# A graph attention kernel: 98 columns of one sum move from GpSimd to VectorE, and the vector loop is written out

## The chip, the cores and the metric

The kernel runs on one core of a Trainium2 chip. The metric is the device time of one execution in microseconds (us), lower is better. It was taken in 3 runs before the change. One more execution was taken with the hardware profiler.

Engines are named as in the profile: PE is the matrix engine (PEld its weight loads), DVE the vector engine, ACT the scalar engine, POOL the GpSimd engine, SP the queue that starts transfers.

## The reference

The model is a two-layer graph attention network followed by a soft mixture of experts. There are 1250 nodes with 768 features, 41250 edges (self loops included), 8 heads of 128 channels in the first attention layer and one head of 768 in the second. The change touches the attention layers alone:

```
def gat_layer(x, W, att_src, att_dst, bias, src, dst, heads, out_ch, concat):
    h = (x @ W.T).reshape(n, heads, out_ch)
    a_src = einsum('nhc,hc->nh', h, att_src)
    a_dst = einsum('nhc,hc->nh', h, att_dst)
    e = leaky_relu(a_src[src] + a_dst[dst], 0.2)
    m = segment_max(e, dst)
    ex = exp(e - m[dst])
    alpha = ex / (segment_sum(ex, dst)[dst] + 1e-16)
    out = segment_sum(alpha[:, :, None] * h[src], dst)
    return out + bias

x = x + gat2(relu(gat1(layernorm(x))))
x = x + soft_moe(layernorm(x))
```

## The kernel before, in words

The kernel makes the attention dense. A first stage counts the edges between every pair of nodes and keeps `ln_c`, the logarithm of the count, with a large negative number where there is no edge: 10 tiles of 128 destination nodes by 1280 source nodes. 1250 nodes are padded to `NP` = 1280, so the last 30 columns of each row belong to no node.

`attend` then runs once for each layer. It has `heads * NT` steps: 80 in the first layer (`gat1`), 10 in the second (`gat2`). One step is one tile of 128 destinations for one head. A step goes through the engines so:

- POOL (L737) adds `s_row`, the source logits of the head spread over all partitions, and the tile's `ln_c`, into `base`, 128x1280.
- ACT (L753) makes `relus`, the part that turns the sum into a leaky ReLU.
- DVE (L783) adds `relus` and `base` into `q` and takes the row maximum in the same instruction; a second short instruction of that line reads the maximum out into `top`. Ahead of it a MEMSET of one column, `gate` (L782), carries the last of the waits. L787 negates `top`.
- ACT (L758) takes the exponential of `q` in place and sums it into `den`. DVE turns the sum into a factor (L806, L810).
- PE (L849) transposes `q` into PSUM as `gat_pt`, ten blocks of 128x128. ACT (L768) and DVE (L798) copy it out as a high and a low fp16 half, `pt_hi` and `pt_lo`.
- PE (L79 to L81) multiplies by the features `h` in three products, `gat_o`. DVE (L818 in the first layer, L830 and L834 in the second) scales it and adds the bias, into `rows`. In the first layer PE transposes `rows` (L854) and ACT (L763) and DVE (L792) write the result as fp16 halves.

All engines run the same counter `k` from -1 to `steps + 2`, each with its own lag. In iteration `k`, POOL, ACT and DVE work on `base`, `relus` and `q` of step `k + 1`; DVE then does the low half of step `k - 1`, the rows of step `k - 2` and the factor of step `k`. `base`, `relus` and `q` have two slots each. POOL may start `base` of step `k + 1` when `q` of step `k - 1` is done:

```
at_least(eng, q_ready, k)
eng.tensor_tensor(base[:, w, :], ..., ALU.add).then_inc(base_ready, 1)
```

The order on every engine is that of the code. It is made short by `rolled`: iterations -1 to 4 are written out, those up to `steps - 2` run in a hardware loop of two iterations a turn (37 turns in the first layer, 2 in the second), and the last four are written out again. In the loop the semaphore values and addresses come from registers, which the engine's own queue works out (`DVEq`, `POOLq` rows in the profile).

Of the kernel before, what the change touches and what calls it, by code (L numbers as in the profile page):

```python
# [24 lines left out]
F32 = mybir.dt.float32  # L25
# [5 lines left out]
ds = bass.ds  # L31
# [38 lines left out]
def at_least(eng, sem, value):  # L70

    if not isinstance(value, int) or value > 0:
        eng.wait_ge(sem, value)
# [567 lines left out]
def attend(nc, mem, sem, const, name, heads, width, ln_c, h, nad, a_rows, bias, turned=None,  # L641
# [8 lines left out]

    steps = heads * NT
    s_row = mem("s_row", [P, 2, NP], F32)
    relus = mem("relus", [P, 2, NP], F32)
    base = mem("base", [P, 2, NP], F32)
    q = mem("q", [P, 2, NP], F32)
    pt = [mem(f"pt_{x}", [P, 2, NT, P], F16) for x in ("hi", "lo")]
    top = mem("top", [P, 2], F32)
    neg_top = mem("neg_top", [P, 2], F32)
    gate = mem("gate", [P, 2], F32)
    den = mem("den", [P, 4], F32)  # L660
    scaled = mem("scaled", [P, 2], F32)
    factor = mem("factor", [P, 2], F32)
# [1 line left out]
    bias_all = mem("bias_all", [P, heads * width], F32)  # L664
    in_bias, bias_ready = sem(f"{name}_in_bias"), sem(f"{name}_bias")
    in_s = sem(f"{name}_in_s")
    relu_ready, base_ready, q_ready = sem(f"{name}_relu"), sem(f"{name}_base"), sem(f"{name}_q")
    neg_ready, p_ready = sem(f"{name}_neg"), sem(f"{name}_p")
    pt_turned, hi_ready, lo_ready = sem(f"{name}_ptt"), sem(f"{name}_hi"), sem(f"{name}_lo")
    out_done, scaled_ready, factor_ready = (  # L670
# [8 lines left out]
    with (  # L679
# [5 lines left out]
        def run(eng, step):  # L685
            rolled(eng, step, -1, 5, steps - 1, steps + 3)
# [7 lines left out]
        @block.sync  # L694
        def _(eng):
            eng.dma_start(bias_all[:, :], bias.to_broadcast([P, heads * width])).then_inc(in_bias, 16)

            def load_s(head, slot):
                at_least(eng, in_s, 16 * head)

                at_least(eng, relu_ready, (head - 1) * NT)
                at_least(eng, base_ready, (head - 1) * NT)
                eng.dma_start(s_row[:, slot, :].rearrange("p (t n) -> p t n", t=NT),
                              a_rows[ds(head * NT, NT), :].unsqueeze(0).to_broadcast([P, NT, P]))\
                   .then_inc(in_s, 16)

            for head in range(min(heads, 2)):
                load_s(head, head)
            if heads > 2:
                with eng.Fori(1, heads // 2) as pair:  # L710
                    for slot in range(2):
                        load_s(2 * pair + slot, slot)
            if residual is not None:
                def load_x(k):
                    eng.dma_start(xs[:, k % 2, :], residual[k * P:(k + 1) * P, :])\
                       .then_inc(in_x[k % 2], 16)

                load_x(0)
                load_x(1)
                for k in range(steps):  # L720
                    eng.wait_ge(rows_ready, k + 1)
                    eng.dma_start(stored[k * P:(k + 1) * P, :], rows[:, k % 2, :])\
                       .then_inc(saved[k % 2], 16)
                    if k + 2 < steps:
                        load_x(k + 2)
                for u in range(2):
                    eng.wait_ge(saved[u], 16 * (steps // 2))

        @block.gpsimd
        def _(eng):  # L730
            def step(k, u):
                if valid(k + 1):
                    w = (u + 1) % 2
                    head, j = head_tile(k + 1)
                    eng.wait_ge(in_s, 16 * (head + 1))
                    at_least(eng, q_ready, k)
                    eng.tensor_tensor(base[:, w, :], s_row[:, ds(head % 2, 1), :],  # L737
                                      ln_c[:, ds(j, 1), :], ALU.add).then_inc(base_ready, 1)
            run(eng, step)

        @block.scalar
        def _(eng):
            eng.wait_ge(in_bias, 16)
            eng.activation(bias_all[:, :], bias_all[:, :], ACT.Copy, scale=out_scale)\
               .then_inc(bias_ready, 1)

            def step(k, u):
                w = (u + 1) % 2
                if valid(k + 1):
                    head, j = head_tile(k + 1)  # L750
                    eng.wait_ge(in_s, 16 * (head + 1))
                    at_least(eng, q_ready, k)
                    eng.activation(relus[:, w, :], s_row[:, ds(head % 2, 1), :], ACT.Relu,  # L753
                                   bias=nad[:, ds(k + 1, 1)], scale=-0.8).then_inc(relu_ready, 1)
                if valid(k):
                    eng.wait_ge(neg_ready, k + 1)
                    at_least(eng, factor_ready, k - 1)
                    eng.activation(q[:, u, :], q[:, u, :], ACT.Exp, bias=neg_top[:, u:u + 1],  # L758
                                   accum_out=den[:, u:u + 1]).then_inc(p_ready, 1)
                if turned and valid(k - 3):  # L760
                    head, j = head_tile(k - 3)
                    eng.wait_ge(rows_turned, k - 2)
                    eng.activation(turned[0][:, ds(head, 1), ds(j * P, P)],  # L763
                                   op[:, w, P:2 * P], ACT.Relu).then_inc(th_ready, 1)
                if valid(k - 1):
                    eng.wait_ge(pt_turned, k)
                    at_least(eng, out_done, k - 2)
                    eng.activation(pt[0][:, w, :, :].rearrange("p t n -> p (t n)"),  # L768
                                   tp[:, w, 0:NP], ACT.Copy, scale=S_PROB).then_inc(hi_ready, 1)
            run(eng, step)  # L770

        @block.vector
        def _(eng):
            eng.wait_ge(bias_ready, 1)

            def step(k, u):
                w = (u + 1) % 2
                if valid(k + 1):
                    eng.wait_ge(relu_ready, k + 2)
                    eng.wait_ge(base_ready, k + 2)  # L780
                    at_least(eng, pt_turned, k)
                    eng.memset(gate[:, w:w + 1], 0.0)  # L782
                    eng.tensor_tensor_reduce(q[:, w, :], relus[:, w, :], base[:, w, :], 1.0, -MASK / 2,  # L783
                                             ALU.add, ALU.max, top[:, w:w + 1]).then_inc(q_ready, 1)
                    eng.wait_ge(q_ready, k + 2)
                    at_least(eng, p_ready, k)
                    eng.tensor_scalar(neg_top[:, w:w + 1], top[:, w:w + 1], -1.0, None, ALU.mult)\  # L787
                       .then_inc(neg_ready, 1)
                if turned and valid(k - 3):
                    head, j = head_tile(k - 3)  # L790
                    eng.wait_ge(th_ready, k - 2)
                    eng.scalar_tensor_tensor(turned[1][:, ds(head, 1), ds(j * P, P)],  # L792
                                             op[:, w, P:2 * P], 0.0,
                                             turned[0][:, ds(head, 1), ds(j * P, P)],
                                             ALU.max, ALU.subtract).then_inc(tl_ready, 1)
                if valid(k - 1):
                    eng.wait_ge(hi_ready, k)
                    eng.scalar_tensor_tensor(pt[1][:, w, :, :].rearrange("p t n -> p (t n)"),  # L798
                                             tp[:, w, 0:NP], S_PROB,
                                             pt[0][:, w, :, :].rearrange("p t n -> p (t n)"),  # L800
                                             ALU.mult, ALU.subtract).then_inc(lo_ready, 1)
                if valid(k - 2):
                    rows_out(k - 2, u)
                if valid(k):
                    eng.wait_ge(p_ready, k + 1)
                    eng.tensor_scalar(scaled[:, u:u + 1], den[:, u:u + 1], S_PROB * S_ACT / out_scale,  # L806
                                      TINY, ALU.mult, ALU.add).then_inc(scaled_ready, 1)
                    eng.wait_ge(scaled_ready, k + 1)
                    at_least(eng, rows_ready, k - 1)
                    eng.reciprocal(factor[:, u:u + 1], scaled[:, u:u + 1]).then_inc(factor_ready, 1)  # L810

            def rows_out(k, u):
# [7 lines left out]
                       .then_inc(rows_ready, 1)  # L820
                else:

                    if isinstance(k, int):
                        eng.wait_ge(in_x[u], 16 * (k // 2 + 1))
                    else:
                        eng.wait_ge(in_x[u], 16 * ((k - u) // 2 + 1))
                    if not isinstance(k, int) or k >= 2:

                        eng.wait_ge(saved[u], 16 * ((k - u) // 2))
                    eng.tensor_tensor(rows[:, u, :], xs[:, u, :], bias_all[:, :], ALU.add)\  # L830
                       .then_inc(sum_ready, 1)
                    eng.wait_ge(sum_ready, k + 1)
# [3 lines left out]
                                             rows[:, u, :].rearrange("p (c n) -> p c n", c=2),  # L836
                                             ALU.mult, ALU.add).then_inc(rows_ready, 1)

            run(eng, step)

        @block.tensor
        def _(eng):
            def step(k, u):
                w = (u + 1) % 2
                if valid(k):
# [748 lines left out]
```

## Time and profile before

| | us |
|---|---|
| median of 3 runs | 2096.01 (2095.04 to 2098.13) |
| the profiled execution | 2098.8 |
| its span, first to last instruction | 2097.0 |
| PE busy | 1781.3 (85%) |
| DVE busy | 1227.6 (59%) |
| ACT busy | 932.2 (44%) |
| POOL busy | 270.6 (13%) |

The span is what the trace covers; 1.8 us of the profiled execution lie around it. The shares are averages over all stages. The first attention layer runs from about 447 to 835 us after the span's start, the second from about 934 to 1075 us, and POOL works nearly only in these two. In a row of the timeline, "idle before <-releaser" is the engine's idle time ahead of the instruction and what ended it; "issue" is idle time for which the profile shows no releaser.

### The profile page before, as it was taken

How to read it: one execution, taken by the hardware profiler on the slowest of the kernel's cores; microseconds unless marked ns; L12 is line 12 of the kernel's file. 1: busy time of each engine (PE TensorE's matmuls, PEld its weight loads, DVE VectorE, ACT ScalarE, POOL GpSimd, SP SyncE). 2: the span in 40 equal slices, each digit the busy share in tenths (PEclk: the TensorE clock that was granted, in tenths of full speed). 3: DMA queues.
4: the chain of work that ended last, by engine and by line, in shares of the span. 5: the costliest groups of instructions: out<-in, count | busy, mean ns of one | idle time of the engine just before them, and what ended most of it. 6: DMA issues, size and time to landing. Idle time of an engine off the chain costs nothing. (4 is left out here: it accounts for less than half of the span.)

```text
span 2097.0 us, 38651 instructions
## 1 busy us (share of the span) xinstructions
PE 1781.3 (85%) x11825; PEld 1097.9 (52%) x11825; DVE 1227.6 (59%) x2013; ACT 932.2 (44%) x1366; POOL 270.6 (13%) x113
## 2 busy tenths in 40 slices
PE   4948878858898887958847979999999996999799
PEld 2413333336777776535533435655656553666455
DVE  6676777778888887435345114555555555666311
ACT  2107767758888886214203113333333333565300
POOL 0000000036666663013000000000000000000000
PEclk9979999979999999988978999999999998999999
DMA  4000000000000000111140001212112123332311
GB/s 156 0 7 0 0 0 0 0 35 13 13 13 25 13 0 26 50 35 46 61 170 26 0 30 62 78 59 76 62 59 79 59 71 123 113 110 74 128 64 50
DMA packets 33674, 104.08 MB, mean 50 GB/s; under 512 B 3286, under 2 KB 3386, under 8 KB 33500
## 3 DMA queue, kind: packets, MB, share of 16 engines
q1 hardware_dynamic: 33564, 103.39, 14.4%
q8 instruction: 28, 0.46, 0.1%
q14 instruction: 18, 0.15, 0.0%
q10 hardware_dynamic: 64, 0.08, 0.0%
HBM read 75.07 MB, written 28.38 MB: 49 GB/s over the span
## 5 line engine op out<-in xcount | busy, mean ns | idle before, releaser
L737 POOL TENSOR_TENSOR base<-s_row,ln_c 128x1280 f32 (+1 forms) x90 | 261.2, 2903 | 609.1 <-DMA s_row<-a_rows 440.5
L631 PE MATMUL ce_c<-one_src,one_dst 128*128 x1053 | 211.6, 347 | 42.7 <-issue 34.9
L574 DVE TENSOR_SCALAR one_src<-iota,src 128x1280 f16 x351 | 171.2, 549 | 69.3 <-PE ce_c L631 62.2
L79 PE MATMUL di_l<-x2t_hi,ph_hi 128*128 128x512 f16 (+1 forms) x576 | 196.4, 341 | 12.4 <-DVE ph_lo L1160 11.0
L80 PE MATMUL di_l<-x2t_lo,ph_hi 128*128 128x512 f16 (+1 forms) x576 | 196.3, 341 | 0.0
L81 PE MATMUL di_l<-x2t_hi,ph_lo 128*128 128x512 f16 (+1 forms) x576 | 196.3, 341 | 0.0
L79 PE MATMUL gat_o<-h_hi,pt_hi 128*128 (+1 forms) x800 | 180.0, 228 | 2.4 <-DVE pt_lo L798 1.9
L631 PEld LDWEIGHTS ce_c<-one_src,one_dst 128*128 x1053 | 101.7, 97 | 152.7 <-issue 92.2
L81 PE MATMUL gat_o<-h_hi,pt_lo 128*128 (+1 forms) x800 | 172.5, 218 | 0.0
L80 PE MATMUL gat_o<-h_lo,pt_hi 128*128 (+1 forms) x800 | 171.8, 218 | 0.0
L849 PE MATMUL gat_pt<-ident,q 128*128 128x128 f32 x900 | 121.1, 284 | 53.9 <-ACT q L758 41.9
L783 DVE CUSTOM_DVE_ANT_0 q<-relus,base 128x1280 f32<-128x1280 f32 x90 | 165.1, 1834 | 0.0
L598 ACT ACTIVATE apart<-iota,minus_dst 128x128 f16 x351 | 115.4, 391 | 71.1 <-PE ce_c L631 37.5
L768 ACT ACTIVATE pt_hi<-gat_pt 128x1280 f16<-128x1280 f32 x90 | 110.8, 1231 | 66.0 <-PE gat_pt L849 66.0
L849 PEld LDWEIGHTS gat_pt<-ident,q 128*128 128x128 f32 x900 | 101.7, 145 | 66.0 <-ACT q L758 43.4
L798 DVE SCALAR_TENSOR_TENSOR pt_lo<-gat_pt,pt_hi 128x1280 f16<-128x1280 f32 x90 | 133.3, 1481 | 1.8 <-ACT pt_hi L768 1.7
L79 PE MATMUL co_c<-ps_hi,hid_hi 128*128 128x305 f16 (+1 forms) x384 | 115.4, 301 | 20.8 <-DVE ps_lo L1387 20.2
L758 ACT ACTIVATE q<-q,neg_top 128x1280 f32<-128x1280 f32 x90 | 122.5, 1361 | 19.5 <-DVE neg_top L787 19.5
L1155 DVE SCALAR_TENSOR_TENSOR pt_lo<-di_t,pt_hi 128x1280 f16<-128x1280 f32 x32 | 47.7, 1492 | 140.5 <-ACT pt_hi L1109 140.5
L753 ACT ACTIVATE relus<-s_row,nad 128x1280 f32 (+1 forms) x90 | 122.4, 1362 | 1.9 <-DMA s_row<-a_rows 1.9
L80 PE MATMUL co_c<-ps_lo,hid_hi 128*128 128x305 f16 (+1 forms) x384 | 115.1, 300 | 0.0
L81 PE MATMUL co_c<-ps_hi,hid_lo 128*128 128x305 f16 (+1 forms) x384 | 115.1, 300 | 0.0
(214 smaller groups left out, 3656.1 us busy)
## 6 DMA issues: line engine op xcount, KB each, us to landing
logits_t<-lg SPq DMA_DIRECT2D x32, 625.0 KB, 3.7
logits_in<-logits_t SPq DMA_DIRECT2D x32, 625.0 KB, 4.0
phf<-in_phi SPq DMA_DIRECT2D x32, 384.0 KB, 3.9
xs<-x SPq DMA_DIRECT2D x20, 384.0 KB, 4.9
s_row<-a_rows SPq DMA_DIRECT2D x9, 640.0 KB, 3.8
ew<-in_fw SPq DMA_DIRECT2D x6, 768.0 KB, 13.1
wf<-in_fw SPq DMA_DIRECT2D x12, 384.0 KB, 6.8
xs<-in_x SPq DMA_DIRECT2D x10, 384.0 KB, 7.4
```

What stands on the lines that cost most here:

```text
L79: eng.matmul(out, lh, rh, start=first, stop=False, skip_group_check=True)
L80: eng.matmul(out, lh, rl, start=False, stop=False, skip_group_check=True)
L81: return eng.matmul(out, ll, rh, start=False, stop=last, skip_group_check=True)
L574: eng.tensor_scalar(one_src[:, ds(slot + i, 1), :], const["iota"][:, :], src[:, ds(block_at + i, 1)], None, ALU.is_equal)\
L598: eng.activation(apart[:, ds(k % 2, 1), i, :], const["iota"][:, j * P:(j + 1) * P], ACT.Abs, bias=minus_dst[:, ds(block_at + i, 1)])\
L631: mm = eng.matmul(cp[:, j % 2, a:a + n], one_dst[:, ds(slot + i, 1), :], one_src[:, ds(slot + i, 1), a:a + n], start=False, stop=False, sk ...
L737: eng.tensor_tensor(base[:, w, :], s_row[:, ds(head % 2, 1), :], ln_c[:, ds(j, 1), :], ALU.add).then_inc(base_ready, 1)
L753: eng.activation(relus[:, w, :], s_row[:, ds(head % 2, 1), :], ACT.Relu, bias=nad[:, ds(k + 1, 1)], scale=-0.8).then_inc(relu_ready, 1)
L758: eng.activation(q[:, u, :], q[:, u, :], ACT.Exp, bias=neg_top[:, u:u + 1], accum_out=den[:, u:u + 1]).then_inc(p_ready, 1)
L783: eng.tensor_tensor_reduce(q[:, w, :], relus[:, w, :], base[:, w, :], 1.0, -MASK / 2, ALU.add, ALU.max, top[:, w:w + 1]).then_inc(q_ready, 1)
L798: eng.scalar_tensor_tensor(pt[1][:, w, :, :].rearrange("p t n -> p (t n)"), tp[:, w, 0:NP], S_PROB, pt[0][:, w, :, :].rearrange("p t n -> ...
L849: mm = eng.transpose(tp[:, u, t * P:(t + 1) * P], q[:, u, t * P:(t + 1) * P], const["ident"][:, :])
```

## The change

In both layers the sum `base` is split: POOL adds columns 0 to 1151 (`POOL_PART` = 9 * 128), DVE adds columns 1152 to 1249, 98 of them, just ahead of its own use of `base` (new line L788). `relus`, `base`, the sum with maximum and the exponential leave the 30 pad columns out. The pads of `q`, which PE still transposes, are set to zero once by POOL, and PE waits for that once. The MEMSET of `gate` is gone. The DVE program of `attend` is no longer looped: all its iterations are written out with constants. The other engines' loops stay. Two slots of `base` and `relus` now lie 1250 columns (5000 bytes) apart, where they were 1280 apart.

```
-    relus = mem("relus", [P, 2, NP], F32)
-    base = mem("base", [P, 2, NP], F32)
+    POOL_PART = (NT - 1) * P
+    relus = mem("relus", [P, 2, N], F32)
+    base = mem("base", [P, 2, N], F32)
...
                 at_least(eng, relu_ready, (head - 1) * NT)
-                at_least(eng, base_ready, (head - 1) * NT)
+                at_least(eng, base_pool, (head - 1) * NT)
+                at_least(eng, base_dve, (head - 1) * NT)
...
         @block.gpsimd
         def _(eng):
+            for u in range(2):
+                eng.memset(q[:, u, N:NP], 0.0).then_inc(pads, 1)
+
             def step(k, u):
...
-                    eng.tensor_tensor(base[:, w, :], s_row[:, ds(head % 2, 1), :],
-                                      ln_c[:, ds(j, 1), :], ALU.add).then_inc(base_ready, 1)
+                    eng.tensor_tensor(base[:, w, 0:POOL_PART], s_row[:, ds(head % 2, 1), 0:POOL_PART],
+                                      ln_c[:, ds(j, 1), 0:POOL_PART], ALU.add).then_inc(base_pool, 1)
             run(eng, step)
+            eng.wait_ge(pads, 2)
...
                 if valid(k + 1):
+                    head, j = head_tile(k + 1)
+                    eng.wait_ge(in_s, 16 * (head + 1))
+                    at_least(eng, q_ready, k)
+                    eng.tensor_tensor(base[:, w, POOL_PART:N], s_row[:, head % 2, POOL_PART:N],
+                                      ln_c[:, j, POOL_PART:N], ALU.add).then_inc(base_dve, 1)
                     eng.wait_ge(relu_ready, k + 2)
-                    eng.wait_ge(base_ready, k + 2)
+                    eng.wait_ge(base_pool, k + 2)
+                    eng.wait_ge(base_dve, k + 2)
                     at_least(eng, pt_turned, k)
-                    eng.memset(gate[:, w:w + 1], 0.0)
-                    eng.tensor_tensor_reduce(q[:, w, :], relus[:, w, :], base[:, w, :], 1.0, -MASK / 2,
+                    eng.tensor_tensor_reduce(q[:, w, 0:N], relus[:, w, :], base[:, w, :], 1.0, -MASK / 2,
                                              ALU.add, ALU.max, top[:, w:w + 1]).then_inc(q_ready, 1)
...
-            run(eng, step)
+            for k in range(-1, steps + 3):
+                step(k, k % 2)
```

The two ACT lines take `0:N` in the same way. In the rows below, `base_4163` is `base` of the first layer, `gat1_base_pool` and `gat1_base_dve` the semaphores of its two parts, `gat1_ptt` the one for PE's transposes, and the two ISA rows are the sum with maximum and the read of the maximum.

DVE, one iteration of the loop of the first layer before:

```order
384 L810 RECIPROCAL factor_4172<-scaled_4171 128x1 [waits gat1_rows,gat1_scaled]
385 L779 REGISTER_ALU
386 L782 MEMSET gate_4169 128x1 [waits gat1_ptt,gat1_base,gat1_relu]
387 L783 ISA q_4164,top_4167<-relus_4162,base_4163 128x1280
388 L783 ISA top_4167 128x1
389 L787 TENSOR_SCALAR neg_top_4168<-top_4167 128x1 [waits gat1_p,gat1_q]
390 L792 ISA [waits gat1_th]
391 L792 REGISTER_ALU
392 L792 SCALAR_TENSOR_TENSOR h1t_lo_86<-gat_o,h1t_hi_85 128x128
```

The same place in the change, written out:

```order
357 L821 RECIPROCAL factor_4171<-scaled_4170 128x1 [waits gat1_rows,gat1_scaled]
358 L788 TENSOR_TENSOR base_4163<-s_row_4161,ln_c_84 128x98 [waits gat1_q,gat1_in_s]
359 L794 ISA q_4164,top_4167<-relus_4162,base_4163 128x1250 [waits gat1_base_dve,gat1_ptt,gat1_base_pool,gat1_relu]
360 L794 ISA top_4167 128x1
361 L798 TENSOR_SCALAR neg_top_4168<-top_4167 128x1 [waits gat1_p,gat1_q]
362 L803 SCALAR_TENSOR_TENSOR h1t_lo_86<-gat_o,h1t_hi_85 128x128 [waits gat1_th]
```

The short sum stands directly ahead of the sum with maximum, which now waits for four semaphores, one of them set by the short sum itself; the register instructions are gone.

POOL, the loop of the first layer in the change (before it reads the same, with L737 and 128x1280):

```order
27 L73 REGISTER_ALU [waits gat1_in_s]
28 L742 ISA [waits gat1_q]
29 L742 ISA
30 L742 TENSOR_TENSOR base_4163<-s_row_4161,ln_c_84 128x1152
31 L740 ISA
32 L742 ISA [waits gat1_q,gat1_in_s]
33 L742 ISA
34 L742 TENSOR_TENSOR base_4163<-s_row_4161,ln_c_84 128x1152
```

Nothing moved here: the same register instructions stand between the wait for `q` and the sum, and the sum is 128 columns shorter.

## Rows read from the trace of the kernel before

**Rows 1.** The page: the span, and all instructions of POOL's sum.
```profile
span 2097.0 us, 38651 instructions
L737 POOL TENSOR_TENSOR base<-s_row,ln_c 128x1280 f32 (+1 forms) x90 | 261.2, 2903 | 609.1 <-DMA s_row<-a_rows 440.5
```
**Rows 2.** Busy time by stretch: the looped part of the first layer (ends with granted clock).
```profile
core 0: us, PE busy (x) PEld busy (x) DVE busy (x) ACT busy (x) POOL busy (x), PEclk, DMA share, GB/s
...
470.00:830.00 360.00, 319.70 (x3194) 261.77 (x3193) 311.62 (x693) 305.32 (x383) 215.97 (x75) 1.00 0.03 11
```
**Rows 3.** Who waited for whom, 470 to 820 us: total us, times, longest.
```profile
POOL base L737 <- DVE top L783: 119.0, 69, 1.8
ACT h1t_hi L763 <- PE gat_o L854: 49.3, 76, 1.1
PE gat_o L854 <- DVE rows L818: 26.0, 74, 2.0
```
**Rows 4.** Timeline of POOL (start us, us, instruction, idle before): fill, loop, last.
```profile
447.71 5.72 POOL L737 TENSOR_TENSOR base<-s_row,ln_c 128x1280 f32<-128x1280 f32 x2 [309.49 <-DMA s_row<-a_rows]
454.94 2.90 POOL L737 TENSOR_TENSOR base<-s_row,ln_c 128x1280 f32<-128x1280 f32 x1 [1.51 <-DVE top L783]
...
472.78 2.90 POOL L737 TENSOR_TENSOR base<-s_row,ln_c 128x1280 f32 x1 [1.74 <-DVE top L783]
...
704.43 2.90 POOL L737 TENSOR_TENSOR base<-s_row,ln_c 128x1280 f32 x1 [1.70 <-DVE top L783]
709.09 2.91 POOL L737 TENSOR_TENSOR base<-s_row,ln_c 128x1280 f32 x1 [1.76 <-DVE top L783]
...
811.10 2.91 POOL L737 TENSOR_TENSOR base<-s_row,ln_c 128x1280 f32 x1 [1.76 <-DVE top L783]
```
**Rows 5.** Timeline of DVE, one iteration of the loop.
```profile
702.48 1.60 DVE L783 CUSTOM_DVE_ANT_0 q<-relus,base 128x1280 f32<-128x1280 f32 x1
704.01 0.08 DVE L783 DVE_READ_ACCUMULATOR2_ANT top<- 128x1 f32 x1
704.12 0.15 DVE L787 TENSOR_SCALAR neg_top<-top 128x1 f32<-128x1 f32 x1
704.65 0.29 DVE L792 SCALAR_TENSOR_TENSOR h1t_lo<-gat_o,h1t_hi 128x128 f32 x1 [0.37 <-issue]
...
706.70 0.16 DVE L810 RECIPROCAL factor<-scaled 128x1 f32<-128x1 f32 x1
706.93 0.06 DVE L782 MEMSET gate<- 128x1 f32 x1
706.97 1.71 DVE L783 CUSTOM_DVE_ANT_0 q<-relus,base 128x1280 f32<-128x1280 f32 x1
708.61 0.08 DVE L783 DVE_READ_ACCUMULATOR2_ANT top<- 128x1 f32 x1
```
**Rows 6.** Timeline of DVE in the fill of the first layer.
```profile
450.82 3.96 DVE L783 CUSTOM_DVE_ANT_0 q<-relus,base 128x1280 f32<-128x1280 f32 x1
454.71 0.08 DVE L783 DVE_READ_ACCUMULATOR2_ANT top<- 128x1 f32 x1
...
454.98 4.21 DVE L783 CUSTOM_DVE_ANT_0 q<-relus,base 128x1280 f32<-128x1280 f32 x1
```
**Rows 7.** Timeline of DVE in the second layer: its rows, and L783 with POOL idle.
```profile
976.92 0.96 DVE L830 TENSOR_TENSOR rows<-res,bias_all 128x768 f32<-128x768 f32 x1 [6.70 <-PE gat_o L81]
...
989.03 0.96 DVE L830 TENSOR_TENSOR rows<-res,bias_all 128x768 f32<-128x768 f32 x1 [6.70 <-PE gat_o L81]
...
991.59 1.49 DVE L783 CUSTOM_DVE_ANT_0 q<-relus,base 128x1280 f32<-128x1280 f32 x1
...
1001.41 0.96 DVE L830 TENSOR_TENSOR rows<-res,bias_all 128x768 f32<-128x768 f32 x1 [6.74 <-PE gat_o L81]
```
**Rows 8.** Timeline of PE there: the transposes behind the last product of a step.
```profile
988.83 1.25 PE L849 MATMUL gat_pt<-ident,q 128*128 128x128 f32 x10
...
1000.94 1.25 PE L849 MATMUL gat_pt<-ident,q 128*128 128x128 f32 x10
```

More of the change, by code:

```diff
@@ L658, in attend @@
     neg_top = mem("neg_top", [P, 2], F32)
-    gate = mem("gate", [P, 2], F32)
     den = mem("den", [P, 4], F32)
@@ L666, in attend @@
     in_s = sem(f"{name}_in_s")
-    relu_ready, base_ready, q_ready = sem(f"{name}_relu"), sem(f"{name}_base"), sem(f"{name}_q")
+    relu_ready, q_ready, pads = sem(f"{name}_relu"), sem(f"{name}_q"), sem(f"{name}_pads")
+    base_pool, base_dve = sem(f"{name}_base_pool"), sem(f"{name}_base_dve")
     neg_ready, p_ready = sem(f"{name}_neg"), sem(f"{name}_p")
@@ L752, in step @@
                     at_least(eng, q_ready, k)
-                    eng.activation(relus[:, w, :], s_row[:, ds(head % 2, 1), :], ACT.Relu,
+                    eng.activation(relus[:, w, :], s_row[:, ds(head % 2, 1), 0:N], ACT.Relu,
                                    bias=nad[:, ds(k + 1, 1)], scale=-0.8).then_inc(relu_ready, 1)
@@ L757, in step @@
                     at_least(eng, factor_ready, k - 1)
-                    eng.activation(q[:, u, :], q[:, u, :], ACT.Exp, bias=neg_top[:, u:u + 1],
+                    eng.activation(q[:, u, 0:N], q[:, u, 0:N], ACT.Exp, bias=neg_top[:, u:u + 1],
                                    accum_out=den[:, u:u + 1]).then_inc(p_ready, 1)
@@ L821, in rows_out @@
                 else:
[L823 to L829, printed above, removed]
+                    eng.wait_ge(in_x[u], 16 * (k // 2 + 1))
+                    if k >= 2:
+                        eng.wait_ge(saved[u], 16 * (k // 2))
                     eng.tensor_tensor(rows[:, u, :], xs[:, u, :], bias_all[:, :], ALU.add)\
@@ L837, in rows_out @@
                                              ALU.mult, ALU.add).then_inc(rows_ready, 1)
-            run(eng, step)
+            for k in range(-1, steps + 3):
+                step(k, k % 2)
         @block.tensor
         def _(eng):
+            eng.wait_ge(pads, 2)
             def step(k, u):
```

## The prediction

> **What bounds the kernel now.** I read the page first for where the changed lines stand. POOL's sum runs 90 times at 2.90 us [rows 1]; over the span POOL is hardly busy, so its share says nothing, and what counts is the stage. In the looped part of the first layer PE, DVE and ACT are each busy for 85 to 89% of 360 us, POOL for 60%, at full granted clock (1.00, the 2.4 GHz level) [rows 2]. No engine is full. The table of waits names the link: POOL waits for DVE's maximum in nearly every step, 119.0 us in all [rows 3], and the timelines show the other half of it.
>
> POOL's starts run from 472.78 to 811.10 us in 73 steps [rows 4], 4.63 us a step. Within one step: DVE reads the maximum at 704.01 [rows 5]; POOL starts 0.42 us later at 704.43 and ends at 707.33 [rows 4]; DVE has issued its sum with maximum already at 706.97, and that ends at 708.68, 1.35 us after POOL's end [rows 5]. Its operand `base` isn't what it waits for. POOL is a step ahead: in the fill DVE issues at 450.82 with its own `base` done and ends at 454.78, while POOL's next sum ran to 453.43; then it issues at 454.98 and ends at 459.19, POOL having run from 454.94 to 457.84 [rows 4, 6]. Each time the end lies 1.35 us after POOL's end, and with POOL idle the instruction takes 1.49 us in all [rows 7]. So a DVE instruction with two SBUF inputs stands still while POOL's sum runs, and POOL's next sum in turn waits for it by a semaphore. The two take turns: 0.42 (or 0.48 in the other half of the loop) + 2.90 + 1.35 - 0.07 = 4.60 (4.66). That chain bounds 79 intervals of the first layer. All else has slack: ACT waits 49.3 us for PE, PE 26.0 us for DVE [rows 3], and DVE arrives 0.36 us (0.25 in the other half) before POOL ends.
>
> **The change, term by term, per step of the first layer.**
>
> (a) POOL adds 1152 columns for 1280. In proportion that is -0.29 us; with a fixed part as large as DVE's (0.16, below) -0.27. I take -0.285.
>
> (b) DVE's cost per column: 1.49 us for 1280 and 0.96 for 768 [rows 7] give 1.04 ns a column and 0.16 us fixed. 30 columns less: -0.03.
>
> (c) The new short sum: alone 0.16 + 98 x 1.04 ns = 0.26 us. It has two SBUF inputs as the sum with maximum has, and it comes to the head of DVE's queue while POOL's sum for the step after runs. So I let it stand still until POOL ends. Behind a wait of that kind the start-up is already paid (1.35 against 1.49), so it ends 0.26 - 0.14 = +0.12 us after POOL. Bounds: 0.12, and 0.26 if it pays its full time.
>
> On that hand-over the trace shows 1280 x 1.04 = 1.33 us of columns in the 1.35 us, so some 0.02 us of handing over [rows 4 to 7]. [...]
>
> (d) The sum with maximum now waits for the short sum's semaphore and only then issues. Before, it stood ready when POOL ended. It pays its start-up in the open: +0.14.
>
> Sum: -0.285 - 0.03 + 0.12 + 0.14 + 0.22 = +0.165 us a step, times 79 = **+13.0 us**. The short sum costs DVE little; it costs the chain more than POOL's tenth gives, since it stands on the chain in series and takes away the head start of the instruction behind it.
>
> (f) Fill: two POOL sums lie ahead of each layer's first maximum, -0.57 us a layer; the first short sum comes between them (0) or after both (+0.48); I take +0.25. Two layers: -0.6. Two more intervals of the second layer's fill go as the first layer's: +0.3. After that PE sets the pace there (12.1 us a step) and POOL and the short sum are covered by it.
>
> (g) The written-out DVE program. In the first layer its register work (0.37 us idle ahead of L792 [rows 5]) and the MEMSET lie where DVE would otherwise stand still behind POOL: 0 us, and were the cover gone they would give at most some 0.4 us a step. In the second layer they are on the path: from the last product's end to L830 it is 0.20 us in a written-out step (988.83 to 989.03) and 0.47 in a looped one (1000.94 to 1001.41) [rows 7, 8]. 4 looped steps: -1.1.
>
> (h) At nothing: 30 columns less in each ACT instruction (covered by ACT's waits for PE, else -0.06 a step); the two pad MEMSETs (POOL waits 309 us for the first transfer [rows 4]); PE's one wait for them; SP's extra semaphore (it refills a slot ten steps ahead of its use); POOL's register work, unchanged.
>
> Total: 13.0 - 0.6 + 0.3 - 1.1 = +11.6. On the profiled execution of 2098.8 that is 2110.4; the profiled one lies 2.8 above the median of 2096.0, so for the median I predict **2107.7**. The bounds of (a), (c) and (e) that I hold likely, (e) from 0.15 to 0.30, give 2102 to 2114.
>
> **Rivals.**
>
> *The short sum doesn't stand still behind POOL* (13%). No row shows a plain TENSOR_TENSOR of DVE beside POOL's sum; only the custom instruction of L783 is seen to stop. Then it and its wait end ahead of POOL (DVE would issue the sum with maximum some 2.99 us after the read of the maximum, POOL ends at 0.42 + 2.62 = 3.04), the turn loses (a) and (b) alone: -0.315 x 79 = -25, with -1.2 in the fills and -1.1 from (g): 2069. It decides as soon as the short sum takes under 0.3 us while POOL runs. For it: its size, and that L787 and L806 run beside POOL unhindered. Against it: these have one input, and L783 has the same two kinds of inputs as the short sum. The Trainium skill (SBUF — State Buffer, "Who interferes with whom") states that a `tensor_tensor` with both inputs in SBUF contends with a GpSimd instruction that reads SBUF and that the later one fully blocks; that speaks for my case, and the trace agrees as far as L783 goes (4.21 us for 1.49).
>
> *The wait is nearly free* (11%). With (e) at 0.03 the step changes by -0.025: -2.0, and -1.4 from (f) and (g): 2092 to 2093, about no change. For it: the 0.03 us behind the read of the maximum. Against: the number of semaphores.
>
> *POOL doesn't gain in one slot* (7%). The odd slot of `base` now starts at 5000 bytes, not 5120; no row shows such a slot. If POOL lost its gain there, 40 steps cost 0.285 more: +11, 2119.
>
> **How the numbers follow.** My case has 69%, the rivals 13, 11 and 7. 0.2% (4.2 us) is about what a measurement of this kernel tells from no change: faster is below 2091.8, slower above 2100.2. Faster: the first rival and 1% of the second, 0.14. Same: the rest of the second and a low tail of 2% of my case, 0.12. Slower: 0.74. The range takes in my case, the second rival and the third: 2092 to 2119; it leaves out the first. My case's own range is 2102 to 2114.
>
> **What would show it.** The step of POOL's starts between 473 and 811 us goes from 4.63 to about 4.80 us. L742 takes 2.62 us. L788 shows far more than 0.26 us and ends 0.12 us after POOL; L794 starts 0.2 us behind it and takes 1.46 us, never more. The second layer's steps are all 12.1 us. I am wrong if L788 takes 0.26 us while POOL runs and L794 is the one that is stretched (then 2069), if the gap between L788 and L794 is under 0.1 us (then about 2093), or if POOL's odd sums are longer than the even ones.

## The result, and the profile after

The median of 5 runs is **2105.23 us** (2102.05 to 2108.16), against 2096.01 us before (five runs by now, 2095.04 to 2098.65): 1.0042 times as long, 95% interval 1.0028 to 1.0057. The profiled execution took 2105.23 us too, with a span of 2103.4 us (2098.8 and 2097.0 before). The forecast was 2107.7 us and slower.

The page of the changed kernel, its span and the two groups of the change:

```profile
span 2103.4 us, 38298 instructions
L742 POOL TENSOR_TENSOR base<-s_row,ln_c 128x1152 f32 (+1 forms) x90 | 237.0, 2634 | 226.8 <-DVE top L794 215.1
L794 DVE CUSTOM_DVE_ANT_0 q<-relus,base 128x1250 f32<-128x1250 f32 x90 | 140.2, 1557 | 21.6 <-DVE base L788 21.6
```

POOL's sum is down from 2.903 us [rows 1] to 2.634. A new link stands in the last line: the sum with maximum waits 21.6 us in all for the short sum, 0.24 us each of 90 times.

Busy time of the same stretch as [rows 2] (PE, PEld, DVE, ACT, POOL, then granted clock, DMA share, GB/s):

```profile
470.00:830.00 360.00, 307.44 (x3039) 251.71 (x3039) 335.23 (x671) 293.29 (x372) 194.82 (x74) 1.00 0.03 11
```

DVE is busy for 93% now, 87% before. That isn't work: an instruction counts as busy while it stands still, and the short sum takes 0.85 us a time in the median where it needs 0.25. PE and ACT, whose work is the same or a little less, fall to 85 and 81%, since the steps are longer. The clock is at 1.00 as before.

All instructions of the short sum, with the shortest, median and longest in ns, and who waited for it:

```profile
L788 DVE TENSOR_TENSOR base<-s_row,ln_c x90: 250/852/2714, 445.0 to 1035.5; 128x98 f32<-128x98 f32 x90
...
  DVE q L794: 21.6, 90
```

Who waited for whom, 470 to 820 us, the answer to [rows 3]:

```profile
POOL base L742 <- DVE top L794: 160.6, 73, 2.2
ACT h1t_hi L769 <- PE gat_o L864: 64.1, 72, 1.2
...
PE gat_o L864 <- DVE rows L829: 39.4, 72, 1.8
DVE q L794 <- DVE base L788: 17.4, 72, 0.2
```

POOL waits longer for DVE: 160.6 us in 73 waits for 119.0 in 69, so 2.2 us a time for 1.7. Its timeline, for [rows 4], fill, loop and last:

```profile
451.67 2.69 POOL L742 TENSOR_TENSOR base<-s_row,ln_c 128x1152 f32<-128x1152 f32 x1 [1.47 <-DVE top L794]
...
701.92 2.62 POOL L742 TENSOR_TENSOR base<-s_row,ln_c 128x1152 f32 x1 [2.17 <-DVE top L794]
706.78 2.65 POOL L742 TENSOR_TENSOR base<-s_row,ln_c 128x1152 f32 x1 [2.23 <-DVE top L794]
...
822.83 2.65 POOL L742 TENSOR_TENSOR base<-s_row,ln_c 128x1152 f32 x1 [2.23 <-DVE top L794]
```

And DVE in one step, for [rows 5]:

```profile
701.50 0.08 DVE L794 DVE_READ_ACCUMULATOR2_ANT top<- 128x1 f32 x1
...
703.72 0.16 DVE L821 RECIPROCAL factor<-scaled 128x1 f32<-128x1 f32 x1
703.82 0.84 DVE L788 TENSOR_TENSOR base<-s_row,ln_c 128x98 f32<-128x98 f32 x1
704.91 1.46 DVE L794 CUSTOM_DVE_ANT_0 q<-relus,base 128x1250 f32<-128x1250 f32 x1 [0.24 <-DVE base L788]
706.30 0.08 DVE L794 DVE_READ_ACCUMULATOR2_ANT top<- 128x1 f32 x1
```

Read the turn off these: the maximum is read at 701.50, POOL starts at 701.92 and ends at 704.54. The short sum, issued at 703.82, ends at 704.66, 0.12 us after POOL. The sum with maximum starts 0.25 us after that, at 704.91, and takes its full 1.46 us; the next read is at 706.30, POOL's next start 0.48 us behind it. 0.42 + 2.62 + 0.12 + 0.25 + 1.46 - 0.07 makes 4.80 us (the read starts 0.07 us before the trace has the sum with maximum ended); the trace has 4.81 and 4.86 in the two halves of the loop, 4.835 on average, where it was 4.635.

Where the 6.4 us between the two spans are. The first layer is taken by POOL's starts; in the second, PE sets the pace, so it ends with the last of DVE's ten sums of residual and bias (L830, now L837), whose first and last start at 964.82 and 1074.83 us before, 972.80 and 1081.75 after:

| stretch | before | after | |
|---|---|---|---|
| to POOL's first sum | 447.71 | 444.99 | -2.7 |
| POOL's first to last sum, first layer | 363.39 | 377.84 | +14.45 |
| to POOL's first sum of the second layer | 123.4 | 121.7 | -1.7 |
| to DVE's first L830 | 30.36 | 28.30 | -2.06 |
| first to last L830 | 110.01 | 108.95 | -1.06 |
| to the end | 1022.2 | 1021.7 | -0.5 |

The first stretch does the same work in every kernel, but for the two short pad MEMSETs; over all the traces of this study its end falls anywhere from 443.0 to 448.6 us. So single traces compare to a few microseconds only, and below the step of the first layer is the measure: the mean distance of POOL's starts in the loop.

### The profile page after: what moved, and what is told of

It reads as the page before. It is cut to its first block and busy times, and to the rows that moved or that the text cites. A ratio compares the mean times of both kernels' runs of the same rounds, so it can differ in the third digit from the quotient of the medians.

```text
span 2103.4 us, 38298 instructions
## 1 busy us (share of the span) xinstructions
PE 1776.2 (84%) x11825; PEld 1096.2 (52%) x11825; DVE 1266.2 (60%) x2013; ACT 927.6 (44%) x1366; POOL 246.8 (12%) x117
## 5 line engine op out<-in xcount | busy, mean ns | idle before, releaser
L742 POOL TENSOR_TENSOR base<-s_row,ln_c 128x1152 f32 (+1 forms) x90 | 237.0, 2634 | 226.8 <-DVE top L794 215.1
L794 DVE CUSTOM_DVE_ANT_0 q<-relus,base 128x1250 f32<-128x1250 f32 x90 | 140.2, 1557 | 21.6 <-DVE base L788 21.6
L764 ACT ACTIVATE q<-q,neg_top 128x1250 f32<-128x1250 f32 x90 | 120.4, 1337 | 20.2 <-DVE neg_top L798 20.2
L759 ACT ACTIVATE relus<-s_row,nad 128x1250 f32 (+1 forms) x90 | 120.2, 1338 | 1.8 <-DMA s_row<-a_rows 1.8
```

Source lines behind the costliest of these rows:

```text
L742: eng.tensor_tensor(base[:, w, 0:POOL_PART], s_row[:, ds(head % 2, 1), 0:POOL_PART], ln_c[:, ds(j, 1), 0:POOL_PART], ALU.add).then_inc(bas ...
L759: eng.activation(relus[:, w, :], s_row[:, ds(head % 2, 1), 0:N], ACT.Relu, bias=nad[:, ds(k + 1, 1)], scale=-0.8).then_inc(relu_ready, 1)
L764: eng.activation(q[:, u, 0:N], q[:, u, 0:N], ACT.Exp, bias=neg_top[:, u:u + 1], accum_out=den[:, u:u + 1]).then_inc(p_ready, 1)
L794: eng.tensor_tensor_reduce(q[:, w, 0:N], relus[:, w, :], base[:, w, :], 1.0, -MASK / 2, ALU.add, ALU.max, top[:, w:w + 1]).then_inc(q_read ...
```

## The experiments

Each kernel was timed against the kernel before on its own chip (2095.14, 2094.73 and 2096.81 us in the three batches), so times are compared by ratio. Each edit is made to the changed kernel; the later ones build on the early short sum and say so.

**No split.** POOL adds all 1250 columns, the short sum and its waits are gone; the written-out DVE program and the left-out pads stay.

```
-    POOL_PART = (NT - 1) * P
+    POOL_PART = N
...
-                    eng.tensor_tensor(base[:, w, POOL_PART:N], s_row[:, head % 2, POOL_PART:N],
-                                      ln_c[:, j, POOL_PART:N], ALU.add).then_inc(base_dve, 1)
```

> The change without the split: POOL adds all 1250 columns, DVE has no short sum; pads left out, gate gone, DVE loop written out as in the change. Theory (the short sum and its wait stand on the turn-taking chain in series): POOL's sum 2.84 us, L788 (sum with maximum) again stretched to end 1.32 us after POOL, step of POOL's starts 4.54 us instead of 4.83, so about 23 us less than the change and 8 to 10 us less than before: 2087. Rival (the written-out loop, the pads or the 5000-byte slots cost the time, not the split): it stays near 2105, steps 4.8 us.

Measured: 2085.14 us, 0.9949 times before (0.9936 to 0.9963); step 4.543 us. Its DVE and POOL in the loop:

```profile
699.95 2.19 DVE L788 CUSTOM_DVE_ANT_0 q<-relus,base 128x1250 f32<-128x1250 f32 x1
702.07 0.08 DVE L788 DVE_READ_ACCUMULATOR2_ANT top<- 128x1 f32 x1
```
```profile
697.98 2.84 POOL L741 TENSOR_TENSOR base<-s_row,ln_c 128x1250 f32 x1 [1.67 <-DVE top L788]
702.55 2.85 POOL L741 TENSOR_TENSOR base<-s_row,ln_c 128x1250 f32 x1 [1.73 <-DVE top L788]
```

The turn of before is back: POOL ends at 700.82, the stretched sum with maximum at 702.14, 1.32 us later. The step is 0.092 us shorter than before, which is the 30 pad columns (0.06 on POOL, 0.03 on DVE). So nothing is left over for the written-out loop, as said. The split is what makes the kernel slower: 1.0042 less 0.9949 is 0.93%, some 19 us.

**The wait carried by the instruction.** The four semaphores of the sum with maximum in another order, nothing else.

```
+                    eng.wait_ge(base_dve, k + 2)
                     eng.wait_ge(relu_ready, k + 2)
                     eng.wait_ge(base_pool, k + 2)
-                    eng.wait_ge(base_dve, k + 2)
```

> The change with its four waits in another order: the wait for the short sum is the one that the sum with maximum carries itself, the other three are taken earlier. Theory (0.25 us from the short sum's end to the next start is the time of two more semaphore instructions): the gap falls to 0.04 to 0.08 us, step 4.64, 15 us less than the change: 2090. Rival (the gap is what DVE needs between dependent instructions of this size, whatever the order): the gap stays 0.25 and the time 2105.

Measured: 2091.16 us, 0.9982 times before (0.9973 to 0.9991); step 4.631 us. DVE there:

```profile
701.53 0.92 DVE L788 TENSOR_TENSOR base<-s_row,ln_c 128x98 f32<-128x98 f32 x1
702.49 1.46 DVE L794 CUSTOM_DVE_ANT_0 q<-relus,base 128x1250 f32<-128x1250 f32 x1
```

**A MEMSET in place of the short sum.** It fills the same 98 columns of `base` with zeros, so the kernel leaves out their sum of logits and log counts.

```
-                    eng.tensor_tensor(base[:, w, POOL_PART:N], s_row[:, head % 2, POOL_PART:N],
-                                      ln_c[:, j, POOL_PART:N], ALU.add).then_inc(base_dve, 1)
+                    eng.memset(base[:, w, POOL_PART:N], 0.0).then_inc(base_dve, 1)
```

> The change with the short sum replaced, in the same place and with the same semaphores, by a MEMSET of the same 98 columns of base, which reads nothing. Left out: the sum of logits and log counts in these 98 columns. Theory (it is the second SBUF input that makes a DVE instruction stand still while POOL's sum runs): the MEMSET takes about 0.1 us beside POOL, the sum with maximum is stretched in its place, step 4.33 us, about 2067. Rival (any DVE instruction on this tile, or one that writes SBUF, stands still behind POOL, or it is the semaphores and not the port): the MEMSET is stretched to POOL's end as L788 was, step 4.7 to 4.8, about 2100.

Measured: 2067.22 us, 0.9873 times before (0.9858 to 0.9888); step 4.344 us.

```profile
703.05 0.14 DVE L788 MEMSET base<- 128x98 f32 x1
703.43 1.62 DVE L793 CUSTOM_DVE_ANT_0 q<-relus,base 128x1250 f32<-128x1250 f32 x1 [0.24 <-DVE base L788]
```
```profile
701.09 2.63 POOL L742 TENSOR_TENSOR base<-s_row,ln_c 128x1152 f32 x1 [1.67 <-DVE top L793]
```

POOL's sum runs to 703.72, and the MEMSET goes through beside it in 0.14 us. The sum with maximum then gets in 0.29 us ahead of POOL's end, the 0.24 us behind the semaphore is hidden, and its end lies 1.33 us after POOL's. So an instruction in the same place with the same semaphores costs nothing here if it doesn't stand still. This is the 2069 us that the first rival priced; what it lacked was the right instruction.

**The short sum early.** In the fill of the changed kernel one step showed a way round:

```profile
451.63 0.25 DVE L788 TENSOR_TENSOR base<-s_row,ln_c 128x98 f32<-128x98 f32 x1
452.05 3.63 DVE L794 CUSTOM_DVE_ANT_0 q<-relus,base 128x1250 f32<-128x1250 f32 x1 [0.17 <-DVE base L788]
```

There the short sum started 0.04 us ahead of POOL (451.67), took 0.25 us, and POOL's sum took 2.69 us, 0.06 more than its mean. In the loop POOL starts 0.42 us or more after the read of the maximum starts, so there is such a gap in every step. The edit puts the short sum of the step after right behind the sum with maximum:

```
+            short(0)
             def step(k, u):
...
                                              ALU.add, ALU.max, top[:, w:w + 1]).then_inc(q_ready, 1)
+                    if valid(k + 2):
+                        short(k + 2)
```

> The same split of 1152 and 98 columns, but DVE does the short sum of step k+2 right behind the sum with maximum of step k+1, ahead of POOL's next start. Theory: it runs in the 0.42 to 0.48 us that POOL needs to start, takes 0.25 us, costs the chain nothing, and the sum with maximum is the one that is stretched behind POOL: step 0.45 + 2.63 + 1.25 = 4.33 us, 0.50 less than the change, 0.30 less than before: 2105 - 39 = 2066 to 2070. Rival (DVE's own program, or ACT and PE, set the step once POOL's turn is short): steps of 4.4 to 4.6, 2075 to 2090.

Measured: 2070.6 us, 0.9875 times before (0.986 to 0.989); step 4.335 us.

```profile
702.05 1.92 DVE L798 CUSTOM_DVE_ANT_0 q<-relus,base 128x1250 f32<-128x1250 f32 x1
703.90 0.08 DVE L798 DVE_READ_ACCUMULATOR2_ANT top<- 128x1 f32 x1
703.90 0.25 DVE L786 TENSOR_TENSOR base<-s_row,ln_c 128x98 f32<-128x98 f32 x1
```
```profile
704.33 2.65 POOL L742 TENSOR_TENSOR base<-s_row,ln_c 128x1152 f32 x1 [1.67 <-DVE top L798]
```

The short sum is over at 704.15, 0.18 us before POOL starts. The same work on the same engine, 0.5 us a step cheaper by its place alone: it doesn't stand still, its semaphore has long come when the sum with maximum asks for it, and the sum with maximum is again issued before POOL ends (697.76, POOL ending at 698.29).

**POOL's loop written out.** 

```
-            run(eng, step)
+            for k in range(-1, steps - 1):
+                step(k, k % 2)
```

> The change with POOL's loop in attend written out too (constants in place of registers). Theory (the 0.42 to 0.48 us from DVE's read of the maximum to POOL's start is on the chain, 0.27 to 0.33 of it POOL's register instructions): POOL starts 0.15 us behind the read as in the fill, step 4.83 - 0.30 = 4.53 us, 22 to 24 us less than the change: about 2082. Rival (another engine takes over, or the gap is not the register work): step stays above 4.75, time above 2098.

Measured: 2090.73 us (one of ten executions took 3668 us, the others 2089.2 to 2094.6; why is not known), 0.9982 times before (0.9973 to 0.9992); step 4.622 us.

```profile
704.79 0.08 DVE L795 DVE_READ_ACCUMULATOR2_ANT top<- 128x1 f32 x1
```
```profile
705.02 2.65 POOL L742 TENSOR_TENSOR base<-s_row,ln_c 128x1152 f32<-128x1152 f32 x1 [1.97 <-DVE top L795]
```

POOL starts 0.23 us after the start of the read, where it was 0.42 and 0.48. The gain is 0.21 us a step and not 0.3: the expectation had set 0.42 from the read's start against 0.15 from its end. POOL's register work between its wait and its sum is thus on the path, at some 0.2 us a step.

**DVE's loop kept.** The split in the form of before: DVE looped with registers, the MEMSET of `gate` back.

```
+                    eng.memset(gate[:, w:w + 1], 0.0)
...
-            for k in range(-1, steps + 3):
-                step(k, k % 2)
+            run(eng, step)
```

> The change with DVE's loop kept as before: 37 turns of two iterations, addresses and waits in registers, and the gate MEMSET back, which the sum with maximum needs to carry a register wait. The split and the pads are as in the change. Theory (writing DVE's program out gives nothing in the first layer, since DVE stands still behind POOL there, and 1 us in the second): the chain gets the MEMSET's 0.04 us back, L788 still arrives just before POOL ends, step 4.87 to 4.95 us; 4 to 8 us above the change, 2109 to 2113. Rival (the written-out program hides more: with register work DVE arrives after POOL has ended): steps over 5.1 us, above 2125. Rival on the other side (writing it out costs time, in fetching code): below 2102.

Measured: 2140.7 us, 1.0216 times before (1.0202 to 1.0231); step 5.241 us. The one expected was wrong, the rival beside it right.

```profile
702.28 0.26 DVE L789 TENSOR_TENSOR base<-s_row,ln_c 128x98 f32 x1 [0.40 <-issue]
702.78 0.06 DVE L795 MEMSET gate<- 128x1 f32 x1 [0.23 <-DVE base L789]
702.82 1.46 DVE L796 CUSTOM_DVE_ANT_0 q<-relus,base 128x1250 f32<-128x1250 f32 x1
...
707.61 0.26 DVE L789 TENSOR_TENSOR base<-s_row,ln_c 128x98 f32 x1 [0.73 <-issue]
```

POOL's sum (699.46, 2.63 us) ended at 702.09. DVE was still at its register work for the short sum, 0.40 us, in the other half 0.73, so the short sum doesn't even stand still; it comes late and runs in the open. Before, this work had POOL's sum as cover. With the split the written-out DVE program is worth 1.0216 less 1.0042, 1.7%, some 36 us; without it the kernel would be 45 us slower than before, not 9.

**How many columns.** The early short sum with 256, 384 and 192 columns (`POOL_PART` = 994, 866, 1058).

> The early short sum with a larger share: POOL 994 columns, DVE 256. Theory: POOL's sum 2.30 us, DVE's 0.42 us ends 0.50 us after the read and holds POOL's start up a little, turn 0.51 + 2.30 + 1.25 = 4.06 us; DVE's own program then needs 4.1 and PE's and ACT's about as much, so the step is 4.1 to 4.2 against 4.33 with 98 columns: 10 to 17 us less, about 2056. Rival (ACT or PE already sets the step at 98 columns): no gain, 2068 to 2072.

> The same with POOL 866 columns and DVE 384. Theory: POOL's turn is 3.9 us and no longer decides; DVE's program, 0.13 us longer than with 256, sets a step of 4.2 to 4.3 us: 5 to 8 us more than with 256 columns, about 2063. Rival (PE or ACT sets the step, not DVE): the same time as with 256 within 2 us.

> The early short sum with 192 columns on DVE, 1058 on POOL. With 256 columns every second step waited 0.41 us for PE's transposes (steps of 4.43 and 4.02 us in turn), with 98 POOL's turn set 4.33. Theory (two bounds: POOL's turn, and in every second step PE): POOL's turn here is 0.44 + 2.43 + 1.25 = 4.12 us, the PE-bound step stays at 4.4 us: mean 4.2 to 4.25, the time of the 256 columns within 2 us, 2058 to 2062. Rival (DVE's length counts with 256 columns): 3 to 6 us less than with 256.

| columns on DVE | time, us | ratio to before | step, us |
|---|---|---|---|
| 98 | 2070.6 | 0.9875 (0.986 to 0.989) | 4.335 |
| 192 | 2055.79 | 0.9808 (0.9791 to 0.9824) | 4.191 |
| 256 | 2060.1 | 0.9828 (0.9812 to 0.9843) | 4.217 |
| 384 | 2064.18 | 0.9854 (0.9837 to 0.9872) | 4.291 |

By ratio 192 and 256 columns are 0.7 and 0.5% below 98; for 384 the intervals overlap, and only the step is shorter, by 0.044 us. With 256 the time expected was 2056 and the measured one lies 4 us above it, since PE sets every second step, as the rows below show; 384 came out as expected. With 192 the expectation (the time of 256 within 2 us) and its rival (3 to 6 us less) aren't told apart: the time is 4.3 us less, but the intervals of the ratios overlap and the step differs by 0.026 us, 2 us in all. With 256 columns the two halves of the loop fall apart, with steps of 4.43 and 4.02 us in turn (4.26 and 4.12 with 192, 4.43 and 4.15 with 384). The long ones have a new wait:

```profile
657.00 1.46 DVE L798 CUSTOM_DVE_ANT_0 q<-relus,base 128x1250 f32<-128x1250 f32 x1 [0.41 <-PE gat_pt L865]
```

DVE now waits for PE's transposes, and once in two steps PE is late by an idle time ahead of them at the turn of its own loop (`PE gat_pt <- issue`, 12.1 us in 36 times in the table of waits, 470 to 820 us). The rows of PE for that step:

```profile
655.51 1.31 PE L865 MATMUL gat_pt<-ident,q 128*128 128x128 f32 x10 [0.32 <-issue]
...
656.77 0.22 PE L79 MATMUL gat_o<-h_hi,pt_hi 128*128 x1
...
659.12 0.22 PE L81 MATMUL gat_o<-h_hi,pt_lo 128*128 x1
```

The 30 products of a step start over 2.35 us (656.77 to 659.12).

**PE's loop written out, with 256 columns.**

```
-            run(eng, step)
+            for k in range(0, steps + 2):
+                step(k, k % 2)
```

> The early short sum with 256 columns, and PE's loop in attend written out. Theory (PE's register work at the loop's turn, 0.34 us ahead of the transposes in every second step, is what DVE's sum with maximum waits for): all steps go to 4.05 to 4.1 us, 10 to 13 us less than 2060: about 2048. Rival (PE's products themselves, or ACT, need 4.2 us; or the much longer PE program starves for code): 2057 or more.

Measured: **2046.09 us** (2044.94 to 2049.27), 0.9767 times before (0.9751 to 0.9783), the shortest of all; step 4.076 us, 4.12 and 4.02 in turn.

```profile
701.67 0.42 DVE L786 TENSOR_TENSOR base<-s_row,ln_c 128x256 f32<-128x256 f32 x1
...
704.35 1.46 DVE L798 CUSTOM_DVE_ANT_0 q<-relus,base 128x1250 f32<-128x1250 f32 x1
```
```profile
702.10 2.31 POOL L742 TENSOR_TENSOR base<-s_row,ln_c 128x994 f32 x1 [1.71 <-DVE top L798]
```

The short sum ends 0.01 us before POOL starts, POOL ends at 704.41, DVE's sum with maximum starts at 704.35 and takes 1.46 us, so it doesn't stand still. The table of waits has 0.8 us for DVE and 0.9 for ACT from 480 to 760 us, and both are busy for 271 of these 280 us, so the pace is now set by the instructions of these two; by which of them isn't shown. PE has time to spare:

```profile
655.08 0.22 PE L79 MATMUL gat_o<-h_hi,pt_hi 128*128 128x128 f16 x1
...
656.70 0.22 PE L81 MATMUL gat_o<-h_hi,pt_lo 128*128 128x128 f16 x1
656.76 1.26 PE L865 MATMUL gat_pt<-ident,q 128*128 128x128 f32 x10
658.98 0.33 PE L870 MATMUL gat_o<-ident,rows 128*128 128x128 f32 x1 [0.96 <-DVE rows L835]
```

The edit did more than was expected of it. The idle time at the loop's turn is gone, and the 30 products of every step now start over 1.62 us (655.08 to 656.70) where they took 2.35, so that PE waits 0.96 us a step for DVE's rows. The time of 2048 us was forecast well, but the 0.34 us at the turn isn't shown to be its cause by itself: no run takes it away and leaves the products as they are. Writing out POOL's loop too, or 192 columns with PE written out, wasn't tried.

## Why the prediction was right

The mechanism is the one predicted, and each step can be put beside a row. The nearness of the total owes something to luck: the first layer lost 14.45 us for 12.7 said, the second gained 3.1 for 1.1 said, and the two errors nearly cancel.

- **(a) POOL's sum**, said -0.285: 2.903 to 2.634 us, -0.269. The fixed part of 0.16 us, which I had read from DVE and given less weight, would have given the -0.27. POOL's means over this study (2.843 at 1250 columns, 2.633 at 1152, 2.31 at 994) bear it out: 2.1 ns a column and about 0.2 us fixed.
- **(c) The short sum stands still until POOL ends, then takes 0.12 us**: right to 0.01, in this kernel and with the other order of waits. Of the 0.12 us, 0.10 are 98 columns at 1.04 ns, so the hand-over from POOL to DVE takes some 0.02 us. The Trainium skill (SBUF — State Buffer, "A bandwidth-pool intuition that's wrong") has some 115 ns for the other direction, GpSimd blocked until DVE's end; no run here shows that one.
- **(b) and (d) The sum with maximum in the open**, said 1.49 - 0.03: 1.46 us, in every step of the loop.
- **(e) The wait**, said +0.22: 0.24 to 0.25. Exchanging the order of the waits shows that it is 0.20 us for where the late semaphore stands and 0.04 for a wait that the instruction carries. The two parts that were added, 0.15 and 0.07, came from other pairs of instructions, POOL behind DVE and MEMSET behind RECIPROCAL; that they fit so well (0.17 us with one wait instruction between, 0.24 with two) wasn't to be counted on.
- **The sum**: +0.165 said, +0.200 measured. (a) was 0.016 too hopeful and (e) 0.025 too low. The sum also counted too many steps: of the 79 intervals three belong to the fill, the first two of them being the -0.57 of (f). The other 76 lost 15.2 us, where +13.0 was said for 79.
- **(f) The fill**: two shorter POOL sums gave -0.55 up to the third start, with the first short sum between them (the case of 0, where +0.25 was taken), and the next step was 0.24 us shorter (4.16 for 4.40), where the short sum slipped in ahead of POOL. That case I hadn't priced. With the 15.2 it makes the +14.45 of the first layer.
- **(g) The written-out DVE program**: nothing in the first layer (the kernel without the split shows it), and the looped steps of the second layer went from 12.4 us [rows 7] to 12.1, as in these rows of DVE:

```profile
984.90 0.96 DVE L837 TENSOR_TENSOR rows<-res,bias_all 128x768 f32<-128x768 f32 x1 [6.33 <-PE gat_o L81]
997.01 0.96 DVE L837 TENSOR_TENSOR rows<-res,bias_all 128x768 f32<-128x768 f32 x1 [6.33 <-PE gat_o L81]
```

  First to last L830 is 110.01 us before, 108.95 or 108.96 in all ten kernels with DVE written out and 111.66 with its loop kept (its four looped steps take 12.4 us again; 1.7 us more lie in its last step, which isn't explained): -1.06 for the -1.1 said. The second layer's fill gave another -2.06, for which (f) had nothing (-0.3 and +0.3). It is 27.4 to 28.9 us in all eleven other kernels, the one with DVE's loop kept (28.7) and the one without the split (28.9) among them, against 30.4 before; so neither of the two explains it, and its cause stays open. What (g) left out is that the split itself takes the cover away: a looped DVE then has register work for the short sum's addresses and waits, and it ends after POOL. The 0.4 us a step named for a lost cover is what the kernel with the loop kept shows (0.41). So the 0 stands only against the kernel before; for the split the written-out program is no side issue.
- **(h)**: POOL's register work was listed at nothing because unchanged, which is right; writing it out shows that it is on the path with 0.2 us a step.

The rest, -2.7, -1.7 and -0.5 us, lies outside these stretches. The first is scatter (443.0 to 448.6 us). Of the -1.7 a part may go with the written-out program: this stretch is 123.4 and 123.9 us in the two kernels with DVE looped, 120.6 to 122.6 in the other ten. Without the rest the traces would differ by 11.3 us, and the forecast was 11.6 (added to 2096.01 it makes 2107.6; the 2107.7 is off by a tenth). The medians differ by 9.2 us; the 2 us between aren't explained.

The rivals: *the short sum doesn't stand still* has the wrong instruction, since at its 90 places it took 0.85 us in the median for 0.25 alone; but a MEMSET in its place does just that, and its price of 2069 was right: 0.9873 of 2096.01 is 2069.4. The Trainium skill (SBUF — State Buffer, "Who interferes with whom") says that an instruction of DVE with at most one SBUF input, outside its 2-port performance modes, doesn't contend with GpSimd; the trace agrees, with 0.14 us for the MEMSET beside POOL. *The wait is nearly free* was wrong for this order of waits and right for the other: it priced 2092 to 2093, and 0.9982 of 2096.01 is 2092.2. *POOL doesn't gain in one slot*: its sums are 2.63 and 2.64 us in turn on average, and 2.90 and 2.91 before, so the slot at 5000 bytes costs nothing, where 0.285 us was priced.

## What to carry to other kernels

And what a hardware loop spends on registers counts by where it stands in the chain: nothing on DVE while POOL's sum covered it, 0.2 us a step on POOL, 0.41 a step on DVE once the split had taken the cover away; so ask it anew after each change.

## What was not expected of the hardware

- The order of the waits is worth 0.20 us a step: 0.24 us from the short sum's end to the next start with the late semaphore named third of four, 0.04 us with it named first.
- A blocked DVE instruction doesn't take its full time after POOL's end: 98 columns ended 0.12 us after it in the changed kernel and with the other order of waits alike, for 0.25 us when run alone.
- A DVE instruction with two SBUF inputs fits ahead of POOL's start with no cost to POOL's sum: with 98 columns (0.25 us) the sum takes 2.62 to 2.65 us, as in the changed kernel. The one in the fill that overlapped POOL's start by 0.21 us made that sum 0.06 us longer, and with 384 columns (657.34, 0.55 us) it overlapped POOL's start (657.76) by 0.13 us and the sum took 2.04 us, for 2.03 on average.
- PE's 30 products of a step start over 2.35 us in its hardware loop and over 1.62 us written out, both at granted clock 1.00.
- Code written out shows hardly a wait in fetching: with PE's and DVE's programs written out the table of waits has none for issue from 480 to 760 us, and the changed kernel has two on DVE, 0.6 us together.
